# Layer 2's edge sums as one pass of 256 columns, high beside low, and wider put matrices in layer 1

## The reference, cut to what matters

```python
# layer 1 (attention over the edges i <- j)
g_sum = g_r[:, :, None, :, :] + g_l[:, None, :, :, :]
e = jnp.einsum('bijhf,f->bijh', jax.nn.leaky_relu(g_sum, SLOPE), w_attn)
...
# layer 2 (a small network on each edge)
hi = jnp.einsum('bsh,hk->bsk', x, W1[:H])
hj = jnp.einsum('bsh,hk->bsk', x, W1[H:])
h = jax.nn.relu(hi[:, :, None, :] + hj[:, None, :, :] + b1)
y = jnp.einsum('bijk,kl->bijl', h, W2) + b2
y = _layernorm(y, gamma, beta)
out = jnp.einsum('bij,bijh->bih', adj, y)
```

## Time and profile before

| | us |
|---|---|
| median of 3 runs | 1752.94 |
| the three runs | 1749.5, 1752.94, 1760.01 |
| the profiled execution, its own time | 1760.14 |
| its span, first to last instruction | 1758.4 |
| of it, PE busy | 1560.7 (89%) |
| DVE busy | 1249.6 (71%) |
| ACT busy | 976.3 (56%) |
| POOL busy | 4.7 (0%) |

### The profile page before, as it was taken

The page is one execution under the profiler, slowest core; times in us unless marked ns, Lnnn a source line. Parts: engine busy times, 40 slices in busy tenths (PEclk is TensorE's granted clock), DMA queues, the critical chain, the costliest instruction groups (busy, mean ns, idle before and its releaser), DMA issues. The chain is left out here.

```text
span 1758.4 us, 32441 instructions
## 1 busy us (share of the span) xinstructions
PE 1560.7 (89%) x9961; PEld 1252.0 (71%) x9961; DVE 1249.6 (71%) x2330; ACT 976.3 (56%) x2551; POOL 4.7 (0%) x24
## 2 busy tenths in 40 slices
PE   3764889999999999999999987799999999999565
PEld 3553467667766777677777666699999999998554
DVE  4885757877778777786777853467666666666788
ACT  2664745555556565565555621566666666665454
POOL 0000000000000000000000000000000000000000
PEclk9996989999999999999999997899999999999786
DMA  3220534333433343333343310867676767671122
GB/s 79 61 72 5 229 138 162 140 139 141 167 154 139 139 173 149 140 139 138 145 168 151 136 76 1 331 242 257 238 253 242 255 237 256 238 257 61 55 72 66
DMA packets 100649, 274.41 MB, mean 156 GB/s; under 512 B 8800, under 2 KB 51424, under 8 KB 100576
## 3 DMA queue, kind: packets, MB, share of 16 engines
q1 hardware_dynamic: 100176, 273.52, 42.6%
q10 hardware_dynamic: 400, 0.00, 0.0%
HBM read 143.46 MB, written 130.02 MB: 156 GB/s over the span
## 5 line engine op out<-in xcount | busy, mean ns | idle before, releaser
L830 DVE TENSOR_TENSOR b_vv<-bank,b_t 128x512 f32<-128x512 f32 (+1 forms) x192 | 113.8, 599 | 181.7 <-ACT b_t L754 179.5
L1133 DVE TENSOR_REDUCE c_var<-c_ysq 128x4 f32<-128x512 f32 (+1 forms) x192 | 114.0, 594 | 116.9 <-ACT c_ysq L1081 95.6
L658 PE MATMUL wide<-b_vv,put_w 128*64 128x512 f32 (+1 forms) x384 | 180.2, 551 | 7.6 <-DVE b_vv L830 5.8
L723 PE MATMUL bank<-b_wt,b_SIT 128*128 128x136 f32 x1280 | 163.8, 284 | 20.6 <-DVE b_SJ L452 14.2
L1023 PE MATMUL wide<-W2c,c_h 128*128 128x128 f32 x1280 | 174.2, 275 | 0.0
L687 PE MATMUL bank<-b_grs,b_SJ 128*128 128x128 f32 x1280 | 170.3, 293 | 4.2 <-ACT b_os L803 4.2
L723 PEld LDWEIGHTS bank<-b_wt,b_SIT 128*128 128x128 f32 x1280 | 156.0, 193 | 24.6 <-DVE b_SJ L452 14.5
L1023 PEld LDWEIGHTS wide<-W2c,c_h 128*128 128x128 f32 x1280 | 169.7, 193 | 4.3
L687 PEld LDWEIGHTS bank<-b_grs,b_SJ 128*128 128x128 f32 x1280 | 165.9, 208 | 9.3 <-issue 5.0
L1053 PEld LDWEIGHTS bank<-c_z,c_SIT 128*128 128x128 f32 x1280 | 154.3, 193 | 5.5 <-DVE c_z L1141 2.3
L1053 PE MATMUL bank<-c_z,c_SIT 128*128 128x128 f32 x1280 | 154.9, 277 | 2.1 <-DVE c_z L1141 2.1
(11 more groups left out here) (212 smaller groups left out, 3182.4 us busy)
## 6 DMA issues: line engine op xcount, KB each, us to landing
si_d<-b_SI SPq DMA_DIRECT2D x64, 640.0 KB, 3.0
sj_d<-b_SJ SPq DMA_DIRECT2D x64, 640.0 KB, 4.0
sit_d<-b_SIT SPq DMA_DIRECT2D x64, 640.0 KB, 4.6
c_SJ<-sj_d SPq DMA_DIRECT2D x64, 640.0 KB, 4.1
c_SI<-si_d SPq DMA_DIRECT2D x64, 640.0 KB, 5.2
c_SIT<-sit_d SPq DMA_DIRECT2D x64, 640.0 KB, 4.2
xin<-in_x_dram SPq DMA_DIRECT2D x16, 256.0 KB, 3.0
ain<-in_adj_dram SPq DMA_DIRECT2D x16, 256.0 KB, 3.4
```

The source lines that it names most:

```text
L658: pe.matmul(out, e.put_w[:, pos % Q, :], vv[:, (pos + k) % 2, 0:width(k)], start=(pos % Q == 0), stop=False)
L723: d = pe.matmul(ring[0][:, 0:W], s.SIT[:, ms, j, :], wt[:, (pos - LAG) % 2, j, :], start=(j == 0), stop=(j == TILES - 1))
L830: v.tensor_tensor(vv[:, b, 0:w], bU[b][:, 0:w], t[:, b, 0:w], ALU.max).then_inc(v_ok, 1)
L1133: v.tensor_reduce(var[:, k, 0:r], ysq[:, k, 0:width(k)].rearrange("p (j f) -> p j f", f=P), AX.X, ALU.add).then_inc(sum_ok, 1)
```

## The change

In layer 1 the put matrices get 128 columns in place of 64 (the other 64 are zero), and the output of `score` takes all 128 rows of `wide`; only the first 64 are read. The tile `t` goes: `slope(k)` writes into `vv`, and `bend(k)` takes the maximum in place. The wait on e_mm moves from `bend` to `slope`, where it takes the place of a wait on v_ok.

In layer 2 the sums use SIT as float32r, and `z` is split into a high part, a float32r copy, and a low part, the rest. ACT makes the high part (`keep_high`, one copy for each chunk) and GpSimd the low one (a subtraction for each chunk), side by side in `zz`, so that each of the ten matmuls has 256 columns. The result takes 256 columns for each graph, 1024 for a batch, in two banks (`duo`); so the gathers have two banks in place of three. At the batch's end ACT copies the low halves to `rest`, DVE adds the high halves to it, and the product with gamma becomes an operation of its own.

ACT's place for the copies is in its order: after rectify(1) the third chunk of the graph before, after root(1) the first chunk, after root(2) the second.

```diff
@@ layer1_packed: tensor, scalar, vector
-                        out = bE[0:2 * H, chunk(k)]
+                        out = bE[:, chunk(k)]
...
                         if inner or 3 * n + k >= 2:
-                            act.wait_ge(v_ok, 3 * n + k - 1)
-                        act.mul(t[:, (pos + k) % 2, 0:width(k)], pair_bank(pos, k)[:, 0:width(k)], SLOPE).then_inc(t_ok, 1)
+                            act.wait_ge(e_mm, 3 * n + k - 1)
+                        act.mul(vv[:, (pos + k) % 2, 0:width(k)], pair_bank(pos, k)[:, 0:width(k)], SLOPE).then_inc(t_ok, 1)
...
-                        if inner or 3 * n + k >= 2:
-                            v.wait_ge(e_mm, 3 * n + k - 1)
                         w, b = width(k), (pos + k) % 2
-                        v.tensor_tensor(vv[:, b, 0:w], bU[b][:, 0:w], t[:, b, 0:w], ALU.max).then_inc(v_ok, 1)
+                        v.tensor_tensor(vv[:, b, 0:w], bU[b][:, 0:w], vv[:, b, 0:w], ALU.max).then_inc(v_ok, 1)
@@ layer2_packed: gpsimd
+                def step(K, pos, inner):
+                    n, b = 8 * K + pos, pos % 2
+                    if inner or 0 <= n < B:
+                        for k in range(CHUNKS):
+                            js = slice(tiles(k).start, tiles(k).stop)
+                            pool.wait_ge(zh_ok, 3 * n + k + 1)
+                            pool.tensor_tensor(zz[:, b, js, P:2 * P], z[:, b, js, :], zz[:, b, js, 0:P].bitcast(F32),
+                                               ALU.subtract).then_inc(zl_ok, 1)
@@ layer2_packed: tensor
-                        if inner or n >= 1:
-                            pe.wait_ge(h_ok, 3 * n + k - 2)
+                        bank = pair_bank(pos, k)
+                        if inner or 3 * n + k >= 2:
+                            pe.wait_ge(h_ok, 3 * n + k - 1)
...
-                        pe.wait_ge(z_ok, 3 * n)
+                        pe.wait_ge(zh_ok, 3 * n)
+                        pe.wait_ge(zl_ok, 3 * n)
...
-                            d = pe.matmul(bO[:, a:a + P], s.SIT[:, (pos - 1) % 4, j, :], z[:, (pos - 1) % 2, j, :],
+                            d = pe.matmul(bO[:, (pos - 1) % Q, :, :], s.SIT[:, (pos - 1) % 4, j, :], zz[:, (pos - 1) % 2, j, :],
                                           start=(j == 0), stop=(j == TILES - 1))
@@ layer2_packed: scalar
+                    def keep_high(n, b, k):
+                        act.wait_ge(z_ok, 3 * n + k + 1)
+                        if inner or n >= 2:
+                            act.wait_ge(o_mm, n - 1)
+                        act.copy(zz[:, b, tiles(k).start:tiles(k).stop, 0:P],
+                                 z[:, b, tiles(k).start:tiles(k).stop, :]).then_inc(zh_ok, 1)
+
+                    if part(n, pos, inner, 1):
+                        act.wait_ge(o_mm, n - 1)
+                        if inner or n > Q + 1:
+                            act.wait_ge(o_read, batches(K, pos) - 1)
+                        act.copy(rest[:, :, :], bO[:, :, 1, :]).then_inc(rest_ok, 1)
                     if A:
                         rectify(0)
                         rectify(1)
+                    if summed(n, inner):
+                        keep_high(n - 1, (pos - 1) % 2, 2)
...
                     if A:
                         root(1)
+                        keep_high(n, pos % 2, 0)
...
                     if A:
                         square(2)
                         root(2)
+                        keep_high(n, pos % 2, 1)
@@ layer2_packed: vector
-                        v.tensor_tensor(s.res[:, :, :], bO[:, :].rearrange("p (q f) -> p q f", f=P),
-                                        e.gam[:, :].unsqueeze(1).broadcast_to([P, Q, P]), ALU.mult).then_inc(o_read, 1)
+                        v.tensor_tensor(s.res[:, :, :], bO[:, :, 0, :], rest[:, :, :], ALU.add).then_inc(o_read, 1)
                     if part(n, pos, inner, 2):
...
+                        q.add(v.tensor_tensor(s.res[:, :, :], s.res[:, :, :],
+                                              e.gam[:, :].unsqueeze(1).broadcast_to([P, Q, P]), ALU.mult))
+                        q.wait()
...
                         if inner or n >= 2:
-                            v.wait_ge(o_mm, n - 1)
+                            v.wait_ge(zl_ok, 3 * n - 3)
                         total(0)
@@ adjacency_stack
-        put_w = sb("put_w", [P, Q, 2 * Q * HEADS])
-        put_m = sb("put_m", [P, Q, 2 * Q * HEADS], F32R)
+        put_w = sb("put_w", [P, Q, P])
+        put_m = sb("put_m", [P, Q, P], F32R)
```

More of the change, by code:

```diff
@@ L918, in layer2_packed @@
         s.SJ = sb("SJ", [P, 4, ECAP], F32R)
-        s.SIT = sb("SIT", [P, 4, TILES, P])
+        s.SIT = sb("SIT", [P, 4, TILES, P], F32R)
         s.xin = sb("xin", [P, 2, P])
@@ L930, in layer2_packed @@
         z = sb("z", [P, 2, TILES, P])
+        zz = sb("zz", [P, 2, TILES, 2 * P], F32R)
+        rest = sb("rest", [P, Q, P])
         bb = sb("bb", [P, Q, P])
@@ L950, in layer2_packed @@
         z_ok = sem("z_ok")
+        zh_ok = sem("zh_ok")
+        zl_ok = sem("zl_ok")
+        rest_ok = sem("rest_ok")
         o_mm = sem("o_mm")
@@ L953, in layer2_packed @@
         seq_c = sem("seq_c")
-        bU = e.banks[0:3]
-        bP = e.banks[3]
-        bO = e.banks[4]
+        bU = e.banks[0:2]
+        bP = e.banks[2]
         bY = e.banks[5:8]
+        bO = e.duo[:, :].rearrange("p (q a f) -> p q a f", q=Q, f=P)
         def gathered(n, inner):
@@ L970, in batches, with pair_bank @@
             return 8 // Q * K + pos // Q
+        def pair_bank(pos, k):
+            return bU[(pos + k) % 2]
         def rounds(K, pos):
@@ L997, in _ @@
                 pool.memset(s.junk[:, :], 0.0).then_inc(s.sq_ok, 1)
+                def step(K, pos, inner):
[6 more added lines that the diff above has]
+                                               ALU.subtract).then_inc(zl_ok, 1)
+                every_step(pool, step, 0)
             @block.tensor
@@ L1007, in gather @@
                         w, cs, r, b = width(k), chunk(k), pos % 4, pos % 2
-                        if inner or n >= 1:
-                            pe.wait_ge(h_ok, 3 * n + k - 2)
[L1010 to L1013, removed]
+                        bank = pair_bank(pos, k)
+                        if inner or 3 * n + k >= 2:
+                            pe.wait_ge(h_ok, 3 * n + k - 1)
+                        pe.matmul(bank[:, 0:w], hi[:, b, 0:P], s.SJ[:, r, cs], start=True, stop=False)
+                        pe.matmul(bank[:, 0:w], lo[:, b, 0:P], s.SJ[:, r, cs], start=False, stop=False)
+                        pe.matmul(bank[:, 0:w], hi[:, b, P:2 * P], s.SI[:, r, cs], start=False, stop=False)
+                        pe.matmul(bank[:, 0:w], lo[:, b, P:2 * P], s.SI[:, r, cs], start=False, stop=True).then_inc(s.u_mm, 1)
                     def mlp(k):
@@ L1073, in rectify @@
                             act.wait_ge(y_mm, 3 * n + k - 2)
-                        act.activation(h[:, k, 0:width(k)], bU[k][:, 0:width(k)], ACT.Relu,
+                        act.activation(h[:, k, 0:width(k)], pair_bank(pos, k)[:, 0:width(k)], ACT.Relu,
                                        bias=e.b1c[:, 0:1]).then_inc(h_ok, 1)
@@ L1145, in step @@
                     i = batches(K, pos) - (2 if pos % Q == 0 else 1)
-                    q = Steps(v, seq_c, 6 * i)
+                    q = Steps(v, seq_c, 7 * i)
                     def own():
@@ L1166, in step @@
                     if part(n, pos, inner, 4):
-                        q.n = 5
+                        q.n = 6
                         q.wait()
@@ L1853, in adjacency_stack @@
         general = sb("general", [P, 1], I32)
-        banks = [pb(f"bank{i}", [P, 512]) for i in range(5)]
+        banks = [pb(f"bank{i}", [P, 512]) for i in range(3)]
+        duo = pb("duo", [P, 2 * 512])
+        banks += [duo[:, 512 * i:512 * (i + 1)] for i in range(2)]
         wide = pb("wide", [P, 3 * 512])
@@ L1881, in adjacency_stack @@
             mk = c0.enter_context(nc.sbuf_tensor("mk", [P, 1], F32))
-            zero = c0.enter_context(nc.sbuf_tensor("zero", [P, Q * 2 * Q * HEADS], F32))
+            zero = c0.enter_context(nc.sbuf_tensor("zero", [P, Q * P], F32))
             bp = c0.enter_context(nc.sbuf_tensor("bp", [P, 3, P], F32))
@@ L2024, in adjacency_stack @@
         e.wide = wide
+        e.duo = duo
         e.banks = banks
```

8 lines of the change are left out of this document (4 added, 4 removed).

## The result

The changed kernel takes 1802.5 us (median of 4 runs, 1795.8 to 1810.8) where the kernel before takes 1751.3 (median of 4), a ratio of 1.026, 95% interval [1.022, 1.030]: slower, by twice what the prediction's single number said, and inside its range (1741 to 1809). The profiled execution is the fastest of the four, 1795.8 us with a span of 1794.1; the other three have a mean granted clock of 0.932 to 0.933 against its 0.941.

A forecast was written before the change was run, and what follows sets the result against it. PE seemed the bound, but in layer 2 a chain through ACT and DVE was almost as long. Against the median of 1753, -38 for layer 1 and +61 for layer 2 gave 1776 us; range 1741 to 1809.

The forecast's parts named there:

- Layer 1, -38: Layer 1's put matrices: 128-column weight loads are hidden, saving 0.84 us a step before DVE's limits, -38 us over 16 batches.
- Both caps: Layer 1: DVE limits the gain to 0.3 us where L723 waits and 0.4 in the residual step, against 0.84 otherwise.
- The sums: Layer 2: ten float32r matmuls take 1.2 us instead of 2.23, PE's work falls by 1.03, but off the longer chain.
- The copies: Layer 2 on ACT: a slot of 0.51 us each, one in the chain every step; +42 us over 63 steps.
- GpSimd beside DVE: Layer 2: DVE's part waits for GpSimd's 0.94 us subtraction in three steps of four, raising layer 2's cost to +61 us.
- The clock: Rival, layer 2: PE's idle time drops the granted clock to 1.2 GHz at each mlp(0), +69, 1845 us; chance 0.12.
- three signs of being wrong: Layer 2: mlp(0)s under 8.3 us apart, GpSimd's subtraction far from 0.94, or the granted clock leaving full speed.
- no collision: Rival, layer 2: GpSimd and DVE run side by side, -38 + 42 = +4, 1757 us; chance 0.25.
- Layer 1 outrunning its caps: Rival: all 64 layer 1 steps gain 0.84, 54 us, and GpSimd and DVE don't collide, 1741 us; chance 0.13.
- exposed wide loads: Rival, layer 1: 128-column weight loads stay exposed at twice the cost, turning gain to loss, 1864 us; chance 0.04.

The follow-up runs named there:

- The control: Changed kernel with layer 2's sums as before, no copies or GpSimd, and new orders of PE, ACT and DVE: 1706.3 us, ratio 0.971.
- all orders: Changed kernel, same work, with layer 2 reordered on PE (last mlp ahead of the sums), ACT (upper copies later) and DVE (parts last): 1671.0 us, ratio 0.951.

## Why the prediction was right in kind and short in size

*Layer 1, -38.* Right, with some luck in the total: -39 by itself (the two medians), -43.6 between the gathers of the profiled execution, of which the steps' own gains are 36 and the rest is the clock's, which the forecast didn't have in layer 1. Both caps are as forecast, and the loads are hidden; the residual step was the one booked too high, 0.3 for 0.4.

*The sums, 1.03 us off PE's work, worth nothing by themselves.* Nearly right: 1.38 in place of the 1.2, so 0.85 off, and none of it reached the step. The control shows it the other way round: with the chain beneath PE's work, 0.66 of the 0.85 reaches the step, and the kernel gains 35 us.

*The copies, 0.51 in the chain of every step.* Right: the slot is 0.51 (1306.95 to 1307.46), the plain step 8.32 us against 8.29 forecast, and moving one copy took 0.50 off each step. With squares and no collision the step is 8.84, not 8.67; the collision hid that.

*GpSimd beside DVE.* The mechanism is right: the part waits for GpSimd's end, in the three kinds of step named, and not in the reduction's. **The step that failed in size is the subtraction's length, "I take two passes, 0.94": it takes 1.29 us**, near the upper bound of 1.4. Its 0.35 more is lessened by 0.07, because the part ends 0.55 behind GpSimd and not 0.62. The steps came out at 9.22 and not 8.95, so 0.27 x some 44 collision steps = 12 us.

*The clock.* Put down as a rival at +69 and counted in the forecast at nothing; it came in part, 15.6 us in the profiled execution: the larger of the two misses, and a term that was put at nothing. The forecast should have given the up to 2 us of idle time in each step a part of that; the nearest row stood there. PE's idle time ahead of mlp(0) is 1.97 in two of four steps of the changed kernel and 2.46 in another, and the clock fell in 13 of 63 steps. With GpSimd's work halved the longest idle time is 1.90, in one step of four, and it fell in 5 steps, each of that kind; with the copy moved 1.93, and it fell in 2, of that kind again. With the parts moved it is 1.60 at most but for one of 1.74, with both moved 1.44 at most, with all orders nearly none, and the clock fell in no step of layer 2. Every fall lies within 1.5 us behind an mlp(0). That speaks for the idle time as the cause, but no run changed it alone, and most idle times of the same length were followed by no fall.

The sum for layer 2 is then 61 + 12 + 16 = 89, less 5 for the first five steps, which have no part yet and took 7.84 to 8.38, and less 1 because the steps before were 7.95 on average and not 7.93: 83, as measured. The medians lie 51 apart and the profiled executions 36, since the one of before was 9 above the median of 1751.3 and that of after 7 below its own. So some 15 of the 27 us between 1776 and 1802.5 can't be read in the traces; the lower granted clock of the other three runs hints at more slowed steps in them, which isn't shown.

Of the three signs of being wrong that the prediction named, two came: GpSimd's subtraction is 1.29 and not 0.94, and the granted clock in layer 2 left full speed. The undisturbed mlp(0)s from the sixth step on are not under 8.3 apart but for one at 8.25.

The Trainium skill (SBUF — State Buffer, "SBUF: two separate sides") has DVE with two SBUF inputs and a GpSimd instruction that reads SBUF exclude each other for the whole instruction. This case's traces agree, with 1.57 against 0.68 us, and with 0.68 unchanged for the reduction. The Trainium skill also says there that whichever starts first holds the pair; the trace with the parts moved shows it the other way round too, GpSimd's two subtractions at 2.94 us behind a DVE part that was 0.01 ahead (1.80 for the first, whose own time is 1.3).

The rivals: no collision (1757) is what the kernel gives once the parts are moved, 1757.8, but the collisions there are moved and not gone, and the copies' share is another, so the agreement is chance. Layer 1 outrunning its caps and exposed wide loads didn't come.

## What to carry to other kernels

An engine at 99% busy with a chain of nearly the same length beneath it gives nothing for a faster instruction, and each instruction put on the chain costs its full slot: here new orders of ACT, DVE and PE together made the halved count of matmuls in the sums pay, and new orders of ACT and DVE alone didn't yet (1735.7 against 1716.8). So lay out the order of every engine for the new lengths first, with what the next step's first matmul waits for at the head of its queue and copies that are needed a step later behind it. Where GpSimd takes over elementwise work, put beside it DVE's reductions and its instructions that read PSUM, and keep those with two SBUF inputs for when GpSimd rests. A single SBUF input isn't enough to be safe: the small multiplication below was held.

## What the runs showed of the hardware

- GpSimd's subtraction of two SBUF tensors, 128x512 float32, takes 1.27 to 1.30 us and 128x256 takes 0.73: at 512 elements, per element 2.8 times the fill of the earlier trace rows, not twice.
- Even a tiny DVE instruction can be held: the 128x4 multiplication L1205, 0.16 or 0.17 us alone, takes 0.60 when it starts inside GpSimd's instruction (1307.42 + 0.60 = 1308.02, and GpSimd's ends at 1308.01). It reads one SBUF tensor. So does the 128x512 reduction, which isn't held, and so does the reciprocal of 128x2, which took 0.15 or 0.16 each of the 64 times that it began inside GpSimd's instruction with all orders changed. The 128x256 product that reads PSUM kept its 0.42 there 64 times.
- The wait lies inside the held instruction's record. A held 512-element instruction of DVE ends 0.54 to 0.55 us after GpSimd's, 0.13 less than its own 0.68. It seems that some of it is done while it waits; no run shows what.
- Weight loads with 64 columns cost 0.26 and 0.29 us a score in the earlier trace rows, and began only with their own matmul; with 128 columns nothing shows, though a load's own record is longer, 0.19 us against 0.13.
